# A GNN and mixture-of-experts block on one core: the experts' up product in three rounded products, its weights split block by block

## The reference

```python
h = xf @ shared_w1 + shared_b1
t = swiglu5(h, ...)                    # clip, sigmoid gate, product
z = t @ shared_w2 + shared_b2
w, idx = top_k(softmax(xf @ gate_w + gate_b), 2);  w = w / sum(w)
he = einsum('nd,edh->enh', xf, expert_w1) + expert_b1
te = swiglu5(he, ...)
oe = einsum('enh,ehd->end', te, expert_w2) + expert_b2
out = x + einsum('ne,end->nd', cw, oe) + z
```

## Time and profile before

| | |
|---|---|
| Median of 3 runs | 909.06 us (907.97 to 909.75) |
| The profiled execution | 910.05 us, span 908.3 us |
| TensorE busy | 811.4 us (89%) |
| VectorE busy | 485.9 us (53%) |
| ScalarE busy | 250.2 us (28%) |
| GpSimd busy | 126.6 us (14%) |
| L1224, experts' up product | 448 records, 155.9 us busy |
| L1272, experts' down product | 168 records, 78.6 us busy |

### The profile page before, as it was taken

One profiled execution on the slowest core, in us unless ns is written; L12 is line 12 of the kernel. 1 busy time (PEld: TensorE's weight loads), 2 busy tenths in 40 slices (PEclk: granted clock), 3 DMA queues, 4 the chain that ended last, 5 costly groups with the idle time before them and its releaser, 6 DMA issues.

```text
span 908.3 us, 12470 instructions
## 1 busy us (share of the span) xinstructions
PE 811.4 (89%) x3696; PEld 583.8 (64%) x3697; DVE 485.9 (53%) x949; ACT 250.2 (28%) x502; POOL 126.6 (14%) x186
## 2 busy tenths in 40 slices
PE   4679699999999986948999958989999999999993
PEld 2555588888888863626888846887655555555551
DVE  6899481441341387899024685896343443434341
ACT  2455241331341103515221313421021222212121
POOL 2000000000000120000000500212123333333321
PEclk9985699999999995979999968979999999999997
DMA  2600000000000010000101102004698859663542
GB/s 112 205 1 2 1 1 1 0 1 1 1 1 1 29 40 9 1 1 1 47 1 53 58 1 92 22 1 176 218 355 248 297 136 367 167 180 57 135 92 32
DMA packets 32156, 71.34 MB, mean 79 GB/s; under 512 B 4254, under 2 KB 4504, under 8 KB 32110
## 3 DMA queue, kind: packets, MB, share of 16 engines
q1 hardware_dynamic: 25838, 56.04, 17.1%
q0 software_dynamic: 6272, 14.68, 8.1%
HBM read 96.53 MB, written 12.72 MB: 120 GB/s over the span
## 4 chain that ended last, share of the span: by engine, by line
PE 70%; DVE 17%; DMA 6%; issue 3%; ACT 2%; SPq 1%; ACTq 0%; DVEq 0%; POOL 0%; POOLq 0%
PE PS L994 20%; PE PS L1224 14%; PE PS L1024 9%; PE PS L1272 7%; PE PS L1117 5%; PE PS L1063 3%; DMA WB<-in_w 3%; PE PS L925 3%; DMA X<-in_x 3%; PE PS L1257 2%; DVE XN L1343 1%; PE PS L1208 1%; DVE ET L1396 1%; DVE ET L1391 1%; ACT CTR L693 1%
## 5 line engine op out<-in xcount | busy, mean ns | idle before, releaser
L994 PE MATMUL PS<-CTR,YH 125*128 125x500 f32 (+1 forms) x480 | 164.1, 357 | 2.3 <-DVE YL L1526 2.3
L994 PE MATMUL PS<-CTR,YL 125*128 125x500 f32 (+1 forms) x480 | 163.6, 356 | 0.0
L1224 PE MATMUL PS<-WB,YF 128*128 x448 | 155.9, 492 | 0.1
L1224 PEld LDWEIGHTS PS<-WB,YF 128*128 128x128 f32 x448 | 80.9, 190 | 65.7 <-issue 20.7
L994 PEld LDWEIGHTS PS<-CTR,YH 125*128 125x128 f32 x480 | 91.5, 191 | 15.5 <-DVE YL L1526 2.6
L994 PEld LDWEIGHTS PS<-CTR,YL 125*128 125x128 f32 x480 | 91.5, 191 | 13.1
L925 PE MATMUL PS<-ET 125*128 125x130 f16 x494 | 66.4, 302 | 21.1 <-DVE ET L1401 17.2
L1272 PE MATMUL PS<-WB,YF 128*128 x168 | 78.6, 605 | 1.6 <-DMA WB<-in_w 0.9
L925 PEld LDWEIGHTS PS<-ET 125*128 125x128 f16 x494 | 43.2, 128 | 45.0 <-DVE ET L1401 22.2
L1553 DVE TENSOR_TENSOR ZL<-PS,ZH 128x500 fp32r<-128x500 f32 (+1 forms) x36 | 21.1, 592 | 90.1 <-ACT ZH L745 90.1
L648 POOL DMA_INDIRECT out<-YF,dest_i x28 | 44.6, 1591 | 73.5 <-ACT YF L891 48.4
(11 more groups left out here) (363 smaller groups left out, 1369.0 us busy)
## 6 DMA issues: line engine op xcount, KB each, us to landing
WB<-in_w SPq DMA_DIRECT2D x28, 1536.0 KB
WB<-in_w SPq DMA_DIRECT2D x28, 768.0 KB
WB<-in_b SPq DMA_DIRECT2D x28, 384.0 KB
X<-in_x SPq DMA_DIRECT2D x1, 2500.0 KB
xn_dram<-XN SPq DMA_DIRECT2D x1, 2500.0 KB
out<-X SPq DMA_DIRECT2D x10, 250.0 KB
WNEXT<-in_W SPq DMA_DIRECT2D x2, 1024.0 KB, 10.1
SR<-in_sw SPq DMA_DIRECT2D x1, 1536.0 KB, 7.8
```

Source lines behind the costliest of these rows:

```text
L994: mm = nc.tensor.matmul(dest, lhs, rhs, start=(t == 0 and h == 0), stop=(t == NT - 1 and h == 1))
L1224: mm = nc.tensor.matmul(PS[:, 2 * k + h, 0:INTER], xgt[:, k, f, :], WB[:, bass.ds(off + (f * H2 + h * INTER), INTER)], start=(f == 0), sto ...
```

## The change

The up product of a block is written as three products of float32r parts. ScalarE rounds the expert's up weights into `W1H` and the turned rows into `XGH`; VectorE subtracts to get `W1L` and `XGL`. This is done for every block, also where the expert stays the same, in halves of 384 columns of each of the four row groups (128 x 1536 elements an instruction). `W1H[1]` lies where tiles 0 to 5 of `X` were, `W1L[1]` where tiles 6 to 9 and the start of the next area were, so ScalarE waits for the first six stores of `X` (`out_head`) and VectorE for the other four (`out_stored`) before block 1's split. The combining table `CWT` and some tables move.

TensorE turns the rows of blocks 0 and 1 between the shared down products (before tiles 6 and 8), and the wait for the tables moves ahead of these products. In the loop `turn_rows` of block b + 1 follows up product b, as before; the loop is cut at another place. VectorE puts the two subtractions of block b + 1 behind `units` of b - 1; ScalarE puts the result of an older block between its two rounding copies. GpSimd has `AHEAD = 5`: four gathers, then gather 4 and 5 before the first scatter.

```diff
-AHEAD = 3
+AHEAD = 5
+HEAD = 6
...
+        W1H = [at("W1H0", R_XN + ROWB - W1B, [128, FT, H2], F32R), at("W1H1", R_X, [128, FT, H2], F32R)]
+        W1L = [at("W1L0", R_YL + ROWB - W1B, [128, FT, H2], F32R), at("W1L1", R_X + W1B, [128, FT, H2], F32R)]
...
-                sp.dma_start(out[t * NP:(t + 1) * NP, :], X[0:NP, t, :]).then_inc(out_stored, 16)
+                sp.dma_start(out[t * NP:(t + 1) * NP, :], X[0:NP, t, :]).then_inc(out_head if t < HEAD else out_stored, 16)
...
...
-            for b in range(AHEAD):
+            for b in range(4):
                 gather(0, b % 2, b)
             pool.wait_ge(zeroed, 16)
             last = last_pair(pool)
-            gather(0, 1, AHEAD)
-            scatter(0, 0)
...
+            def pair(i):
+                gather(i, 0, i * 2)
+                if not (isinstance(i, int) and i * 2 < AHEAD):
+                    scatter(1, i * 2 - AHEAD)
+                gather(i, 1, i * 2 + 1)
+                scatter(0, i * 2 + 1 - AHEAD)
...
+            def rows_hi(k, b):
+                act.wait_ge(xt_ps, b + 1)
+                nc.scalar.copy(XGH[:, k, :, :], PS[:, 4, :].rearrange("p (f n) -> p f n", f=FT)).then_inc(xgt_hi, 1)
+
+            def split_hi(i, k, b, h):
+                off = act.value_load(eb_i[0:1, 1, bass.ds(b, 1)], min_val=0, max_val=(NWB - 1) * WBUF)
+                cols = slice(h * INTER, (h + 1) * INTER)
+                act.wait_ge(w1_in[k], i * 32 + 32)
+                if not (isinstance(b, int) and b < 2):
+                    act.wait_ge(hb_ready, b - 1)
+                raw = WB[:, bass.ds(off, FT * H2)].rearrange("p (f n) -> p f n", f=FT)
+                nc.scalar.copy(W1H[k][:, :, cols], raw[:, :, cols]).then_inc(w1_hi, 1)
+
+            def pair(i):
+                rows_hi(0, i * 2)
+                sigmoid(0, i * 2 - 2)
+                split_hi(i, 0, i * 2, 0)
+                if not (isinstance(i, int) and i < 2):
+                    result(1, i * 2 - 3)
+                split_hi(i, 0, i * 2, 1)
+                turn_t(0, i * 2 - 2)
...
+            split_hi(0, 0, 0, 0)
+            split_hi(0, 0, 0, 1)
+            rows_hi(0, 0)
+            rows_hi(1, 1)
+            act.wait_ge(out_head, 16 * HEAD)
+            split_hi(0, 1, 1, 0)
+            split_hi(0, 1, 1, 1)
+            pair(1)
...
+                    pe.wait_ge(w1_lo, b * 2 + (h + 1))
                     for f in range(FT):
-                        mm = nc.tensor.matmul(PS[:, 2 * k + h, 0:INTER], xgt[:, k, f, :],
-                                              WB[:, bass.ds(off + (f * H2 + h * INTER), INTER)],
-                                              start=(f == 0), stop=(f == FT - 1))
+                        for j, (x, wt) in enumerate(((XGH, W1H), (XGL, W1H), (XGH, W1L))):
+                            mm = nc.tensor.matmul(PS[:, 2 * k + h, 0:INTER], x[:, k, f, :], wt[k][:, f, cols],
+                                                  start=(f == 0 and j == 0), stop=(f == FT - 1 and j == 2))
...
+            for t in range(NT):
+                if t in (6, 8):
+                    turn_rows(0, t // 8, t // 8)
+                shared_down(t)
+            up(0, 0, None)
             pe.wait_ge(z_added, EARLY)
+            def pair(i):
+                turn_rows(i, 0, i * 2)
+                if not (isinstance(i, int) and i < 2):
+                    down(i - 2, 1, i * 2 - 3)
+                up(1, i * 2 - 1, lambda: turn_act(0, i * 2 - 2))
+                turn_rows(i, 1, i * 2 + 1)
+                down(i - 1, 0, i * 2 - 2)
+                up(0, i * 2, lambda: turn_act(1, i * 2 - 1))
...
-                v.tensor_copy(xgt[:, k, :, :], PS[:, 4, :].rearrange("p (f n) -> p f n", f=FT)).then_inc(xgt_ready, 1)
+                v.tensor_tensor(XGL[:, k, :, :], PS[:, 4, :].rearrange("p (f n) -> p f n", f=FT), f32(XGH[:, k, :, :]),
+                                ALU.subtract).then_inc(xgt_ready, 1)
...
+                v.tensor_tensor(W1L[k][:, :, cols], raw[:, :, cols], f32(W1H[k][:, :, cols]), ALU.subtract
+                                ).then_inc(w1_lo, 1)
...
+            for t in range(1, 4):
                 z_add(t, t)
+            split_lo(0, 0, 0)
+            z_add(4, 4)
+            split_lo(0, 0, 1)
+            z_add(5, 5)
+            rows_lo(0, 0)
+            z_add(6, 6)
+            z_add(7, 7)
+            rows_lo(1, 1)
+            for t in range(8, NT):
+                z_add(t, t)
+            dve.wait_ge(out_stored, 16 * (NT - HEAD))
+            split_lo(1, 1, 0)
+            split_lo(1, 1, 1)
+            def pair(i):
+                units(0, i * 2 - 2, lambda: rows_lo(0, i * 2))
+                split_lo(0, i * 2, 0)
+                split_lo(0, i * 2, 1)
...
```

More of the change, by code:

```diff
@@ L654, in _ @@
             last = last_pair(pool)
-            gather(0, 1, AHEAD)
-            scatter(0, 0)
-            with pool.Fori(2, NB // 2) as i:
-                with pool.If(i < last + 1):
-                    gather(i, 0, i * 2)
-                    scatter(1, i * 2 - AHEAD)
-                    gather(i, 1, i * 2 + 1)
-                    scatter(0, i * 2 + 1 - AHEAD)
-            ending = pool.value_load(eb_i[0:1, 3, 1:2], min_val=SURE - AHEAD, max_val=NB - AHEAD)
+            def pair(i):
[4 more added lines that the diff above has]
+                scatter(0, i * 2 + 1 - AHEAD)
+            pair(2)
+            with pool.Fori(3, NB // 2) as i:
+                with pool.If(i < last + 1):
+                    pair(i)
+            end = ending(pool)
             for j in range(AHEAD):
-                scatter((j + 1) % 2, ending + j)
+                scatter((j + 1) % 2, end + j)
             pool.wait_ge(scattered, pool.to_reg(last * 32 + 32))
@@ L885, in sigmoid, with result @@
                                      ).then_inc(gate_sig, 1)
-            def result(i, k, b, first=False):
+            def result(k, b):
                 act.wait_ge(y_done, b + (EARLY + 1))
-                if not first:
+                if not isinstance(b, int):
                     act.wait_ge(scattered, act.to_reg(b * 16 - 16))
+                elif b >= 2:
+                    act.wait_ge(scattered, b * 16 - 16)
                 nc.scalar.activation(yo[:, k, :], PS[:, 6 + k, :], ACT.Copy,
@@ L895, in _ @@
             last = last_pair(act)
-            sigmoid(0, 0)
-            turn_t(0, 0)
-            sigmoid(1, 1)
-            result(0, 0, 0, first=True)
-            with act.Fori(1, NB // 2) as i:
-                with act.If(i < last + 1):
-                    turn_t(1, i * 2 - 1)
-                    sigmoid(0, i * 2)
-                    with act.If(i < 2):
-                        result(0, 1, 1, first=True)
-                    with act.If(i > 1):
-                        result(i - 1, 1, i * 2 - 1)
-                    turn_t(0, i * 2)
-                    sigmoid(1, i * 2 + 1)
-                    result(i, 0, i * 2)
@@ L911, in _ @@
-            turn_t(1, last * 2 + 1)
-            result(last, 1, last * 2 + 1)
+            def rows_hi(k, b):
[9 more added lines that the diff above has]
+                nc.scalar.copy(W1H[k][:, :, cols], raw[:, :, cols]).then_inc(w1_hi, 1)
@@ new lines, in pair @@
+            def pair(i):
[6 more added lines that the diff above has]
+                turn_t(0, i * 2 - 2)
+                rows_hi(1, i * 2 + 1)
+                sigmoid(1, i * 2 - 1)
+                split_hi(i, 1, i * 2 + 1, 0)
+                result(0, i * 2 - 2)
+                split_hi(i, 1, i * 2 + 1, 1)
+                turn_t(1, i * 2 - 1)
@@ new lines, in _ @@
+            split_hi(0, 0, 0, 0)
[6 more added lines that the diff above has]
+            pair(1)
+            pair(2)
+            with act.Fori(3, NB // 2) as i:
+                with act.If(i < last + 1):
+                    pair(i)
+            end = ending(act)
+            sigmoid(0, end + 3)
+            result(1, end + 2)
+            turn_t(0, end + 3)
@@ L915, in _ @@
+            sigmoid(1, end + 4)
+            result(0, end + 3)
+            turn_t(1, end + 4)
+            result(1, end + 4)
         @block.tensor
@@ L1206, in turn_rows @@
                 pe.wait_ge(gathered[k], i * 16 + 16)
+                if not (isinstance(b, int) and b < 1):
+                    pe.wait_ge(xgt_ready, b)
                 for f in range(FT):
@@ L1962, in _ @@
             shared_act(8)
-            for t in range(1, NT - 1):
+            for t in range(1, 4):
                 z_add(t, t)
-            rows_copy(0, 0)
-            z_add(NT - 1, NT - 1)
-            rows_copy(1, 1)
-            units(0, 0, lambda: None)
-            units(1, 1, lambda: rows_copy(0, 2))
-            with dve.Fori(1, NB // 2) as i:
-                with dve.If(i < last + 1):
-                    units(0, i * 2, lambda: rows_copy(1, i * 2 + 1))
-                    def next_rows():
-                        with dve.If(i < last):
-                            rows_copy(0, i * 2 + 2)
-                    units(1, i * 2 + 1, next_rows)
```

(13 more changed lines are left out.)

70 lines of the change are left out of this document (34 added, 36 removed).

## The result

| | before | changed |
|---|---|---|
| Median | 908.23 us (907.05 to 910.16) | 914.26 us (912.87 to 918.96) |
| Ratio of the runs | | 1.0068, 95% interval 1.0051 to 1.0085 |
| The profiled execution | 910.05 us, span 908.3 | 913.54 us, span 911.2 |

The changed kernel is 0.7% slower, 6 us; the forecast was 901.4 us, its range ended at 911, and its chance for slower was 0.17.

What follows compares the result with a forecast made beforehand. TensorE was taken to bound the experts' stage. Block 2's up product at 678.7, 25 periods of 7.83 and 4.65 end the last up product at 879.1 against 886.76, 7.7 us earlier: 901.4 us, range 896.5 to 911.

Steps and rivals of the forecast that it cites:

- Part 1: TensorE's up product in rounded form: halves of 2.11 us, minus 0.94 us a block, cycle 8.74 to 7.80 us.
- Rival C: Up product isn't shorter because a 190 ns weight load sets TensorE's pace: block 8.14 us, time 909; chance 0.03.
- Part 2: Weight split added to ScalarE (5.45 us a block) and VectorE (7.49 us); a period of 7.83 us taken.
- queued work showed that overlap: Neighbouring instructions on one engine overlap, 0.1 us off at four seams: VectorE-ScalarE loop 7.6 us instead of 7.96.
- Rival A: VectorE-ScalarE loop sets the period because seams don't overlap: 7.96 to 8.1 us a block, 906.9 us; chance 0.13.
- Part 3: Experts' start waits for the stores of X until 664: plus 17 us, block 2's up product at 678.7.
- the allowance for a clock that comes back midway: At the experts' start, TensorE's clock partly low after idling: block 2's up product at 678.7, between 677.3 and 682.
- The 128 GB/s: Queue rate from 642 on, by which ten stores of X take 20 us, from 642 to 663.
- Rival D: Start costs less, stores of X ending at about 658 instead of 664: 895.4 us; chance 0.07.
- Part 4: Rows turned earlier and gathers ahead of scatters, on TensorE, VectorE and GpSimd queues: costed at nothing.
- the tail has the same steps in the same order: Stretch behind the last up product, 21.5 us in the span, taken as unchanged.
- Rival B: GpSimd and VectorE hold each other up: period up to 10.2 us, plus 50 us or so; chance 0.17.

Runs made afterwards that it cites:

- e3: Changed kernel with only register loads moved on ScalarE (one a block, ahead of the sigmoid's wait) and VectorE, dynamic loop kept: 909.3 us, ratio 0.9996.
- e8: Changed kernel with one more register load per block on VectorE, its value unused: 931.84 us, ratio 1.0243.
- e7: Changed kernel with the edits of e2, e3 and e4, dynamic loops kept, VectorE's loop edge placed between a block's two subtractions: 889.21 us, ratio 0.9785.
- e10: Kernel before the change, with its loops written out for 28 blocks: 908.79 us, ratio 1.0003.
- e2: Changed kernel with each store of X issued in two pieces, of 112 and 13 rows: 904.15 us, ratio 0.9938.
- e9: Changed kernel with each scatter put ahead of the gather that it followed on GpSimd: 925.58 us, ratio 1.0171.
- e4: Changed kernel with its loop bound at 14 pairs instead of 18, so no empty iterations: 912.32 us, ratio 1.0039.
- e12: Kernel of e7 with the copy of a scatter's places moved ahead of the wait for the scatter before: 885.05 us, ratio 0.9738.
- e5: Changed kernel with e1, e2 and e3 together, registers also carried over the pair's edge: 891.79 us, ratio 0.9804.
- e11: Kernel of e5 without GpSimd's copies into the index tiles, transfers taking their places from the tables: 883.71 us, ratio 0.9715.
- e1: Changed kernel with the loops over pairs of blocks written out for 28 blocks: 905.58 us, ratio 0.9964.

## Why the prediction was wrong, step by step

**Part 1, right.** A half takes 2.11 us and TensorE's own cycle 7.57 where nothing holds it up, 0.23 below the 7.80 forecast: the down product takes 2.58 instead of 2.71, the two halves with the turn between them 0.1 less together. Rival C (a weight load sets the pace) did not occur.

**Part 2, the durations right, the period wrong.** This is the step that failed: "queued work showed that overlap", and under Rival A "those run on the sequencer while 1.76 us of subtraction are under way". It was true of the steps but not of their sum: the period of 7.83 came out as 8.28 in the loop. Behind the second subtraction stand two register loads of 0.6 to 0.7 us each, and in every second block a loop's edge: 1.67 and 2.1 us beside the 1.68 between two starts. The load ahead of ScalarE's first copy lies in the path too: from the start of the sigmoid to that of the copy it is 0.82 us in the loop (758.97 to 759.79) and 0.55 in e3 (739.84 to 740.39). With the other loads that e3 moves this is worth 0.4 us, by the difference between e3's 7.65 and the loop's 8.03 to 8.09; no run takes them apart. Even the written-out pairs took 7.74, which is this loop and not TensorE's 7.57. I had no row for a register load and should have bounded it; I named it and gave it nothing. Rival A was the mechanism, at 8.28 instead of 7.96 to 8.1. e8 (a load more: +15.9 us), e3, e7 (the same loads elsewhere) and e10 (the same loop under a longer TensorE) show it from four sides.

**Part 3, right but for the clock.** Block 2's up product starts at 677.3, the forecast's early end, for 678.7. The clock was at the lower level as foreseen, granted 0.61 between 666 and 672 us, but only the first half of block 1's up product fell into it, and that was hidden under the activations for which TensorE waited; from 672 to 676 it was granted 1.00. So the allowance for a clock that comes back midway was too much by 1.4 us. The 128 GB/s were read from the first two microseconds and didn't hold (174 between 642 and 650 us before), so it was the landing time read from the trace that carried this part, and not the sum of ten stores. The stores landed where they did before, so Rival D did not occur, and e2 shows that this start is worth 11.8 us.

**Part 4, one term right without a reason, one left out.** "I cost it at nothing" holds for the changed kernel: no turn of rows waits for a gather there between 700 and 860 us. But that was luck. The forecast took the order of gather and scatter to be free, and with one scatter more ahead of each gather it costs 9.4 us (e9). The order of before (`AHEAD = 3`) was not run in the changed kernel. And the loop's end was left out: "the tail has the same steps in the same order" held from the last up product on (20.0 us), but the exit ahead of it cost 3.7 us, some 2.2 of them by empty iterations (e4). Before, the last period shows no such gap (8.66 us), since the last two blocks' bias additions both stood inside the loop. The exit came in the tail, and e10, which has none, takes the same 21.2 us from its last bias addition to the end.

**Rival B, contention, half right.** VectorE's subtraction was never stretched (1.758 us), GpSimd's side was: scatter 1.591 to 1.883, copy of the places 0.191 to 0.540 in the mean between 700 and 860 us. One such copy in the changed kernel's timeline, with the subtraction beside it:

```profile
744.40 1.76 DVE L1899 TENSOR_TENSOR W1L<-WB,W1H 128x1536 fp32r<-128x1536 f32 x1 [0.32 <-ACT W1H L928]
744.89 1.32 POOL L657 COPY dest_i<-RT 128x1 int32 x1 [1.32 <-DMA out<-YF,dest_i]
```

The copy ends at 746.21, 0.05 us behind the subtraction; with no subtraction beside it a copy mostly takes 0.18. Two others, at 764.01 and 813.71, take 1.17 and 0.88 us with 1.12 and 0.84 left of the subtraction. The Trainium skill (SBUF — State Buffer, "Who interferes with whom") says that a VectorE instruction with two SBUF inputs contends with a GpSimd instruction that reads SBUF; the trace agrees, with GpSimd the one that waits. By itself this hardly made the changed kernel slow: the chain of waits shown above goes from bias addition to bias addition without touching GpSimd, and no result of ScalarE waits for a scatter between 700 and 860 us. No run took the contention alone out of the changed kernel. It shows once the rest is gone: the chain of scatters costs 4.3 us in e7 (e12), and with the gathers' copies 8.1 us in e5 (e11). How much of these is contention, and how much the copies' own time and hand-over, was not taken apart.

**The sum.** Forecast 879.1 for the end of the last up product, measured 891.2: start 1.4 earlier, two written-out periods 0.2 shorter, loop 9.9 longer, its end 3.7 longer, which is 12.0 of the 12.1 us. Against before, the block gained 0.46 us (8.74 to 8.28) where 0.91 were forecast, and 25 of them, less the exit, could not pay for a start 16 us later: the last up product ends 4.4 us later. The shorter tail gives back 1.5, so the spans differ by 2.9 us. That is no gain of the change: in the profiled execution before the last down product ran mostly at the lower clock level (granted 0.61 from 892.5 to 896.9), in that of the changed kernel at the higher one (TensorE's timelines, before and changed):

```profile
892.42 4.53 PE L1272 MATMUL PS<-WB,YF 128*128 x6 [0.72 <-ACT YF L877]
```
```profile
896.80 2.84 PE L1326 MATMUL PS<-WB,YF 128*128 x6 [0.75 <-ACT YF L895]
```

In e1, e2, e3, e4 and e7, with the same tail, it took 4.41 to 4.53 us, in e12 2.84. The rest of the 6.0 us between the medians is mostly the spread of executions: the one profiled was 1.8 above its median before and 0.7 below it after.

## What to carry to other kernels

When a faster engine hands the bound to a loop of others, add up what their queues must do between two issues: register loads, address arithmetic, branches, waits. What of that sum is longer than the instruction it hides under is added to the period; move the loads behind a long instruction's issue and put the loop's edge between two long instructions. A wait for a slow transfer, a gather behind a waiting scatter, and iterations that do nothing cost nothing as long as nobody waits for them, so look at them again whenever the bound moves.

## What the runs showed of the hardware

In the changed kernel a register load from SBUF takes 0.28 us on ScalarE and 0.30 on VectorE, its arithmetic 0.15 and 0.19, and with its bounds check and gaps 0.5 us of ScalarE's queue and 0.6 to 0.7 of VectorE's. It is not always so short. Of the loads of L922, L1895, L1904 and L1905 in the changed kernel from 690 us on, eleven took over 0.4 us, up to 1.07, and eight of these are among the twelve that started within 0.4 us of a gather's start on GpSimd. The loop's longest period, 8.67 us, holds one: ScalarE's load at 750.47 took 0.92 us, and the rounding copy behind it started 1.57 us after the sigmoid where 0.82 is usual. Here the whole stage's loads of L1895 in the changed kernel (min, median, max in ns) show the spread:

```profile
L1895 DVEq TENSOR_LOAD <-eb_i x56: 298/307/1066, 633.2 to 877.2; - x56
```

That the gathers cause it is only inferred from their times; no run tested it.

At the loop's end TensorE stood for 2.74 us and its next down product ran at the lower clock level in part (granted 0.75 between 879.5 and 886.2 us, 4.48 us in the record below, for 2.74 elsewhere, TensorE's timeline of the changed kernel). In e2 and e8, with gaps of 2.68 and 2.96 us, the same product took 4.38 and 4.50; in e3, with a gap of 2.60, it took 2.84, and in e4, with hardly a gap, 2.84 too.

```profile
882.35 4.48 PE L1326 MATMUL PS<-WB,YF 128*128 x6 [2.74 <-issue]
```
